# One-hot comparison between gapped layouts, six value buffers and earlier turned blocks in a graph-network kernel

## The chip, the cores and the metric

The kernel runs on one core of a Trainium2 chip. The metric is device time in microseconds (us) of the whole launch, as the median of several executions. Engines are named as the profile names them: PE is the matrix engine, PEld its weight load, DVE the vector engine, ACT the scalar engine, POOL the GpSimd engine, SP the engine that here only issues transfers. SPq and ACTq are transfers issued from SP and ACT.

## The reference, cut to what matters

Four graph layers follow one another on a graph of N = 3125 nodes (feature width 256) and E = 50000 edges. Each layer sums messages over the edges and is followed by a residual and a layer norm. What the change touches is the preparation for them and the first layer's aggregation:

```python
# layer 0: two weighted sums over the edges
a_in  = segment_sum(feat_in[src]  * iw[:, None], dst, num_segments=N)
a_out = segment_sum(feat_out[dst] * ow[:, None], src, num_segments=N)
# layers 1..3 of the second part: the edge attributes summed by destination
e_msg = edge_attr @ We[l].T + be[l]
agg   = segment_sum(x[src] + e_msg, dst, num_segments=n) * inv_deg
```

The kernel never walks the edges in the layers. It first builds an N x N matrix of cells (edge count, summed `iw`, summed `ow`) in memory and a 128 x N sum of the split edge attributes in PSUM. After that every layer is a dense product with that matrix.

## The kernel before, in words

**Scatter stage.** The 50000 edges are 391 tiles of 128 edges (one per partition), taken in chunks of EC = 8 tiles. For each tile ACT compares cell numbers with the neighbouring tiles (`distance`, `equal`), PE finds which edge leads its cell and sums the weights (`claim`, `sums`), and DVE turns eight tiles' sums into values and addresses (`values`, L1299 to L1302). POOL then issues one indirect transfer per tile that adds 128 three-number values to cell_mat (L504); it waits for the landing of the transfer two before. The values lie in VALS = 4 buffers: `values(c)` waits until the scatters of chunk c - 4 have landed.

Edge attributes are summed beside this, LAG = 8 * LAG_C = 40 tiles behind. For tile t, DVE writes a one-hot row per edge (`one_hot`, L1314): 3125 two-byte numbers compared with the edge's destination, into one of three buffers. PE multiplies the 128 attribute columns with it in seven matrix products, one for each 512 columns of the result (`attributes`, L880). ACT and DVE split the attributes of a chunk into a high and a low half (L609, L1308), and `earlier` (L1290) prepares a mask. On each engine all of this is one program in order, so a DVE that waits in `values` writes no one-hots meanwhile.

Before the first one-hot, DVE needs the largest edge attribute: at t = PEAK_SLOT it reads all attributes once in 14 loads (L1332, L1333), and at SCALE_SLOT it forms the scale.

The comparison reads `iota16` through a 125 x 25 view and writes `onehot` through a 25 x 125 view. Both are contiguous, and the profile shows each as one row of 3125.

**Weighted pass.** It starts when every scatter has landed and the attribute sums have been copied from PSUM (`s_ready`). The matrix is read in seven column ranges r (six of 500 columns, one of 125) and 25 row tiles t, 175 steps n. For each step:

- SP loads the cells (L372) into one of three buffers; the load of step n + 3 waits for `lo_ready` of step n. It also stores the counts (L379).
- ACT writes the high half of the weights (`hi_ready`, L651), DVE the low half (`lo_ready`, L1380), POOL casts the counts (L513).
- PE does `in_part` (six products L924 and one L927 for the degrees) and `turns` (eight transposes of blocks into PSUM, L935); `step_done` comes after the last of them.
- ACT copies the turned blocks out of PSUM into `outw` (`turned`, L642).

Every four steps (at t % 4 == 3 and at the last t) a group of turned blocks is complete, and in the next step PE runs `out_part`, a burst of 24 products (L910) on `outw`. DVE adds its result (`added`, L1360 or L1363). There is one `outw`. In program order, ACT does hi(n) and then turned(n - 1); PE does in_part(n), out_part of the pending group, turns(n).

**Later stages.** They are dense products with the count matrix (L1030) and small projections (L978) from about 2100 us on. The change does not touch them.

Of the kernel before, what the change touches and what calls it, by code (L numbers as in the profile page):

```python
# [7 lines left out]
F16 = mybir.dt.float16  # L8
# [3 lines left out]
ALU = mybir.AluOpType  # L12
ACT = mybir.ActivationFunctionType
AX = mybir.AxisListType

P = 125
EPS = 1e-5
WIDE = 4
# [10 lines left out]
def build_gnn(nc, x, src, dst, edge_attr, edge_w, edge_w2, gamma0, beta0, W_in, b_in, W_out, b_out, W_x2i, b_x2i,  # L29
              W_h2h, Wl, bl, Wr, We, be, W_pre, b_pre, W1, b1, W2, b2, W_post, b_post, W3, b3, gamma3, beta3, out):  # L30
    N, D = x.shape
    NT = N // P
# [3 lines left out]
    ET = EM + 1  # L36
    CH = -(-ET // EC)
    in_chunk = lambda c: min(EC, ET - EC * c)
    COLS = WIDE * P
    LAYERS = Wl.shape[0]  # L40
    RANGES = [(r * WIDE, min(WIDE, NT - r * WIDE)) for r in range(-(-NT // WIDE))]
    NR = len(RANGES)
# [13 lines left out]

    LAG_C = 5
    LAG = EC * LAG_C
    VALS = 4
    AHEAD = EC + 4  # L60
    PEAK_LOADS = 13
    PEAK_TILES = EM // PEAK_LOADS
    PEAK_SLOT, SCALE_SLOT = 30, 31

    IN_STEPS = [(r, t) for r in range(NR) for t in range(NT)]
    NS = len(IN_STEPS)
# [22 lines left out]
    with ExitStack() as ctx:  # L89
# [127 lines left out]
        qo = XW + 8 * P  # L217
        iota16 = Q[:, qo:qo + (N + 1) // 2].bitcast(F16)[:, 0:N]
        qe = qo + (N + 1) // 2
        src_i, dst_i = (Q[:, qe + i * ETP:qe + (i + 1) * ETP].bitcast(I32) for i in range(2))  # L220
# [12 lines left out]
        before = [Q[:, qe + s * EC * 64:qe + (s + 1) * EC * 64].bitcast(BF16).rearrange("p (k n) -> p k n", k=EC) for s in range(2)]  # L233
        OH = (N + 1) // 2
        onehot = [AR[:, s * OH:(s + 1) * OH].bitcast(F16)[:, 0:N] for s in range(3)]
        peak_buf = [AR[:, s * PEAK_TILES * EA:(s + 1) * PEAK_TILES * EA] for s in range(2)]
# [5 lines left out]
        apart = [AR[:, ao + s * 192:ao + (s + 1) * 192].bitcast(BF16) for s in range(2)]  # L242
        attr_acc = [psum[:, b, 0:min(512, N - 512 * b)] for b in range(-(-N // 512))]
        ded = lambda c: psum[:, 7, (c % 2) * 128:(c % 2) * 128 + 128]
# [224 lines left out]
        def _(pool):  # L469
# [12 lines left out]
            pool.wait_ge(S["iota_ready"], 1)  # L482
            pool.tensor_copy(iota16, iota_f).then_inc(S["iota_ready"], 1)

# [32 lines left out]
        def _(act):  # L517
# [117 lines left out]
            act.wait_ge(S["attr_done"], ET)  # L635
            act.activation(SA[:, 0:2048].rearrange("p (b n) -> p b n", b=4), psum[:, 0:4, :], ACT.Copy, scale=unscale_a).then_inc(S["s_ready"], 1)

            def turned(n):
                r, t = IN_STEPS[n]
                nt, tt = RANGES[r][1], t % WIDE  # L640
                act.wait_ge(S["step_done"], n + 1)
                act.activation(outw[:, 0:nt, :, tt * P:(tt + 1) * P], turn[n % 2][:, 0:nt], ACT.Copy).then_inc(S["turned"], 1)  # L642
                if t == NT - 1:
                    c0, w = RANGES[r][0] * P, nt * P
                    act.activation(ain[:, :, c0:c0 + w], in_acc[:, :, 0:w], ACT.Copy, scale=unscale0).then_inc(S["in_read"], 1)
            for n, (r, t) in enumerate(IN_STEPS):
                w = RANGES[r][1] * P
                act.wait_ge(cells_in[n % 3], 32 * (n // 3 + 1))
                if n >= 3:
                    act.wait_ge(S["step_done"], n - 2)  # L650
                act.activation(split[n % 3][:, 0, :, 0:w], cells[n % 3][:, 0:3 * w].rearrange("p (n c) -> p c n", c=3)[:, 1:3],  # L651
                               ACT.Copy, scale=scale0[0:P, 1:2]).then_inc(S["hi_ready"], 1)
                if n:
                    turned(n - 1)
            turned(NS - 1)

# [124 lines left out]
        def _(pe):  # L781
# [91 lines left out]
            def attributes(t):  # L873
                c, k = divmod(t, EC)
                if k == 0:
                    pe.wait_ge(S["attr_lo"], c + 1)
                pe.wait_ge(S["onehot_ready"], t + 1)
                own_attr = attr16[c % 2][:, k].rearrange("p c a -> p (c a)")
                for b, a in enumerate(attr_acc):
                    last = pe.matmul(a, own_attr, onehot[t % 3][:, 512 * b:512 * b + a.shape[1]], start=t == 0, stop=t == ET - 1, skip_group_check=True)  # L880
                last.then_inc(S["attr_done"], 1)
# [47 lines left out]
            def turns(n):  # L929
                r, t = IN_STEPS[n]  # L930
                if n >= 2:
                    pe.wait_ge(S["turned"], n - 1)
                for k in range(RANGES[r][1]):
                    for c in range(2):
                        last = pe.transpose(turn[n % 2][:, k, c], split[n % 3][:, c, 1, k * P:(k + 1) * P], ident16[0:P, 0:P])  # L935
                return last
# [5 lines left out]
            for n, (r, t) in enumerate(IN_STEPS):  # L942
                pe.wait_ge(S["lo_ready"], n + 1)
                if t == 0:
                    if pending is not None:
                        out_part(pending)
                    turns(n)
                    in_part(n).then_inc(S["step_done"], 1)
                else:
                    in_part(n)  # L950
                    if pending is not None:
                        out_part(pending)
                    turns(n).then_inc(S["step_done"], 1)
                pending = None
                if t % WIDE == WIDE - 1 or t == NT - 1:
                    pending = groups
                    groups += 1
# [188 lines left out]
        def _(dve):  # L1146
# [164 lines left out]
            def one_hot(t):  # L1311
                if t >= 3:
                    dve.wait_ge(S["attr_done"], t - 2)
                dve.tensor_scalar(onehot[t % 3].rearrange("p (a b) -> p a b", a=N // P), iota16.rearrange("p (a b) -> p a b", a=P), dst_c[:, t:t + 1], None,  # L1314
                                  ALU.is_equal).then_inc(S["onehot_ready"], 1)

# [33 lines left out]
            dve.wait_ge(S["attr_done"], ET)  # L1350
            dve.tensor_scalar(SA[:, 2048:3072].rearrange("p (b n) -> p b n", b=2), psum[:, 4:6, :], unscale_a, None, ALU.mult)
            dve.tensor_scalar(SA[:, 3072:N], psum[:, 6, 0:N - 3072], unscale_a, None, ALU.mult).then_inc(S["s_ready"], 1)

# [23 lines left out]
            for n, (r, t) in enumerate(IN_STEPS):  # L1377
                w = RANGES[r][1] * P
                dve.wait_ge(S["hi_ready"], n + 1)
                dve.scalar_tensor_tensor(out=split[n % 3][:, 1, :, 0:w], in0=cells[n % 3][:, 0:3 * w].rearrange("p (n c) -> p c n", c=3)[:, 1:3],  # L1380
                                         scalar=scale0[0:P, 1:2], in1=split[n % 3][:, 0, :, 0:w], op0=ALU.mult, op1=ALU.subtract).then_inc(S["lo_ready"], 1)
                if (t % WIDE == 1 and t > 1) or (t in (0, 2) and r):
                    added(done)
                    done += 1
                if t == 0 and r:
                    dve.wait_ge(S["step_done"], n)
                    degree(r - 1, False)
# [202 lines left out]
```

## Time and profile before

| What | Value |
|---|---|
| Median of 3 runs | 3545.93 us (3543.48 to 3553.56) |
| The profiled execution's own time | 3530.15 us |
| Its span | 3528.4 us |
| Granted PE clock over the span | 0.893 |
| Busy: PE, DVE, ACT, POOL | 2604.3, 1387.0, 1246.5, 941.1 us |
| Scatter stage, one-hots running | 433.0 to 1349.1 us |
| Weighted pass, six ranges of 500 columns | 1349.1 to about 2056 us |

Starts are microseconds from the start of the span. No engine is busy for most of the span, so the table says little by itself; what matters is what each stage waits for.

### The profile page before, as it was taken

The numbers are of one execution on the slowest core, as the hardware profiler recorded it, in microseconds if no ns is written. First come the engines' busy times: TensorE is split into PE (matmuls) and PEld (weight loads), VectorE is DVE, ScalarE is ACT, GpSimd is POOL, SyncE is SP. The second block draws the span as 40 slices with busy tenths as digits, with TensorE's granted clock in tenths as the row PEclk, the third lists the DMA queues.
The fourth block names the chain that finished last, engine by engine and source line by source line (L and its number), as shares of the span: only waits on it lengthen the run. The fifth ranks groups of instructions, "written<-read, shape, count | busy, mean of one in ns | idle before, by whom it ended". The sixth has DMA issues, their size and how long they took to land. (4 is left out here: it accounts for less than half of the span.)

```text
span 3528.4 us, 36950 instructions
## 1 busy us (share of the span) xinstructions
PE 2604.3 (74%) x14593; PEld 1401.2 (40%) x14593; DVE 1387.0 (39%) x1848; ACT 1246.5 (35%) x2535; POOL 941.1 (27%) x611
## 2 busy tenths in 40 slices
PE   1540096766666775777777769799899996999896
PEld 1310042333332332434444434356555663555543
DVE  2440775545554562444444444401212224133313
ACT  0135195555555514555555541200101112112203
POOL 3000487777777783222222210000000000000000
PEclk9875598888888898999999989899999997999997
DMA  9999633232232226777777752443444424554362
GB/s 377 400 393 396 177 75 53 43 53 43 43 51 45 34 13 144 191 182 186 176 188 193 190 126 68 105 102 80 107 95 93 86 52 104 121 104 105 74 143 74
DMA packets 326008, 466.24 MB, mean 132 GB/s; under 512 B 106089, under 2 KB 261992, under 8 KB 325604
## 3 DMA queue, kind: packets, MB, share of 16 engines
q1 hardware_dynamic: 246445, 420.30, 45.0%
q0 software_dynamic: 57360, 0.92, 4.3%
q10 hardware_dynamic: 22023, 42.59, 3.3%
q8 instruction: 117, 1.92, 0.2%
q14 instruction: 63, 0.52, 0.0%
HBM read 313.97 MB, written 149.75 MB: 131 GB/s over the span
## 5 line engine op out<-in xcount | busy, mean ns | idle before, releaser
L504 POOL DMA_INDIRECT cell_mat<-ROW x391 | 753.0, 1926 | 565.8 <-DMA cell_mat<-SA 322.7
L1030 PE MATMUL psum<-FR 125*128 125x500 f16 (+1 forms) x4200 | 825.9, 355 | 40.5 <-DVE FR L1531 20.8
L880 PE MATMUL psum<-AR,Q 128*128 128x512 f16 (+1 forms) x2737 | 638.3, 385 | 247.0 <-DVE AR L1314 244.1
L1030 PEld LDWEIGHTS psum<-FR 125*128 125x128 f16 x4200 | 388.3, 98 | 451.8 <-issue 69.1
L880 PEld LDWEIGHTS psum<-AR,Q 128*128 128x128 f16 x2737 | 254.4, 104 | 542.3 <-DVE AR L1314 254.3
L1314 DVE TENSOR_SCALAR AR<-Q,ROW 128x3125 f16<-128x3125 f16 x391 | 417.1, 1082 | 94.7 <-PE psum L880 85.6
L924 PE MATMUL psum<-Q,FR 125*128 125x500 f16 (+1 forms) x1050 | 252.1, 381 | 180.9 <-DVE Q L1380 180.9
L1380 DVE SCALAR_TENSOR_TENSOR Q<-Q,small 125x1000 f16<-125x1000 f32 (+1 forms) x175 | 252.4, 1446 | 290.0 <-ACT Q L651 289.7
L1447 DVE SCALAR_TENSOR_TENSOR Q<-psum,small,ROW 128x1000 f32<-128x1000 f32 (+1 forms) x42 | 48.2, 1148 | 747.8 <-PE psum L1030 747.8
L513 POOL CAST Q<-Q 125x500 f16<-125x500 f32 (+1 forms) x175 | 160.4, 916 | 593.5 <-DMA Q<-cell_mat 589.5
L978 PE MATMUL psum<-wl,Q 128*125 128x256 f32 (+1 forms) x1100 | 286.8, 401 | 5.7 <-ACT Q L696 3.0
L642 ACT ACTIVATE Q<-psum 125x1000 f16<-125x1000 f16 (+1 forms) x175 | 160.6, 918 | 326.1 <-PE psum L935 318.2
L651 ACT ACTIVATE Q<-Q,small 125x1000 f16<-125x1000 f32 (+1 forms) x175 | 260.1, 1486 | 44.3 <-DMA Q<-cell_mat 44.1
L586 ACT ACTIVATE AR<-AR,ROW 128x384 bf16<-128x384 f32 x391 | 235.1, 601 | 12.3 <-DMA AR<-cell_rows 11.8
L978 PEld LDWEIGHTS psum<-wl,Q 128*125 128x125 f32 x1100 | 197.7, 188 | 62.4 <-issue 25.5
L910 PE MATMUL psum<-Q,FR 125*128 125x500 f16 (+1 forms) x1050 | 208.9, 354 | 10.0 <-ACT Q L642 6.9
L626 ACT ACTIVATE ROW<-psum 128x1 f32<-128x1 f32 x391 | 63.0, 161 | 420.6 <-PE psum L856 416.1
L924 PEld LDWEIGHTS psum<-Q,FR 125*128 125x128 f16 x1050 | 93.7, 105 | 276.7 <-DVE Q L1380 197.6
L594 ACT ACTIVATE AR<-AR 128x384 bf16<-128x384 bf16 x391 | 198.6, 508 | 0.0
L684 ACT ACTIVATE Q<-psum 128x1000 f32<-128x1000 f32 (+1 forms) x35 | 32.0, 914 | 377.5 <-PE psum L1057 377.5
L910 PEld LDWEIGHTS psum<-Q,FR 125*128 125x128 f16 x1050 | 96.1, 98 | 113.7 <-issue 12.9
L935 PEld LDWEIGHTS psum<-ident,Q 125*125 125x125 f16 x1250 | 106.9, 149 | 64.1 <-issue 39.4
(271 smaller groups left out, 2354.6 us busy)
## 6 DMA issues: line engine op xcount, KB each, us to landing
cell_mat<-SA SPq DMA_DIRECT2D x39, 3000.0 KB, 31.4
Q<-cell_mat SPq DMA_DIRECT2D x150, 703.1 KB
FR<-count_mat SPq DMA_DIRECT2D x180, 585.9 KB
AR<-cell_rows ACTq DMA_DIRECT2D x47, 640.0 KB
count_mat<-Q SPq DMA_DIRECT2D x150, 117.2 KB
AR<-in_edge_attr SPq DMA_DIRECT2D x13, 960.0 KB, 4.7
Q<-in_edge_attr SPq DMA_DIRECT2D x48, 256.0 KB
cell_mat<-ROW POOLq DMA_INDIRECT x391
```

Of the source, the lines that this page charges most:

```text
L504: pool.indirect_dma_start(out=cell_mat, out_offset=bass.IndirectOffsetOnAxis(ap=at[c % VALS][:, k:k + 1], axis=0), in_=vals[c % VALS][:, k ...
L586: act.activation(apart[t % 2].rearrange("p (j n) -> p j n", j=3), rows[c % 2][:, k:k + 3], ACT.Abs, bias=cell_neg[:, t:t + 1]).then_inc(S[ ...
L594: act.activation(same[c % 3][:, k], apart[t % 2].rearrange("p (j n) -> p j n", j=3), ACT.Relu, bias=1.0, scale=-1.0).then_inc(S["eq_done"], 1)
L642: act.activation(outw[:, 0:nt, :, tt * P:(tt + 1) * P], turn[n % 2][:, 0:nt], ACT.Copy).then_inc(S["turned"], 1)
L651: act.activation(split[n % 3][:, 0, :, 0:w], cells[n % 3][:, 0:3 * w].rearrange("p (n c) -> p c n", c=3)[:, 1:3], ACT.Copy, scale=scale0[0 ...
L880: last = pe.matmul(a, own_attr, onehot[t % 3][:, 512 * b:512 * b + a.shape[1]], start=t == 0, stop=t == ET - 1, skip_group_check=True)
L910: last = pe.matmul(out_acc[:, hh, 0:ws], feat[1][:, t0 + k, c, f], outw[:, k, d, 0:ws], start=k == 0 and q == 0, stop=k == nt - 1 and q == ...
L924: pe.matmul(in_acc[:, hh, 0:w], feat[0][:, t, c, f], split[n % 3][:, d, 0, 0:w], start=t == 0 and q == 0, stop=t == NT - 1 and q == 2, ski ...
L978: last = pe.matmul(o, a[:, k * P:(k + 1) * P], wt, start=q == 0, stop=bias is None and q == len(ops) - 1)
L1030: last = pe.matmul(a[:, hh, 0:w], parts[:, c, t, f], slot(m, j)[:, i_, :], start=t == 0 and c == 0, stop=t == NT - 1 and c == 1, skip_grou ...
L1314: dve.tensor_scalar(onehot[t % 3].rearrange("p (a b) -> p a b", a=N // P), iota16.rearrange("p (a b) -> p a b", a=P), dst_c[:, t:t + 1], None,
L1380: dve.scalar_tensor_tensor(out=split[n % 3][:, 1, :, 0:w], in0=cells[n % 3][:, 0:3 * w].rearrange("p (n c) -> p c n", c=3)[:, 1:3], scalar ...
```

## The change

It has four parts.

1. `iota16` is laid out as 125 rows of 25 numbers with a pitch of 26, and each `onehot` buffer as 25 rows of 125 numbers with a pitch of 126. The comparison reads one and writes the other in one instruction of the same 3125 elements. The views can no longer be taken as one row. PE reads the one-hots as rows of 125, so its seven products have 500, ..., 500, 125 columns in place of 512, ..., 512, 53, and the copies out of PSUM follow.
2. VALS goes from 4 to 6 and LAG_C from 5 to 6 (LAG from 40 to 48 tiles).
3. PEAK_SLOT and SCALE_SLOT go from 30, 31 to 37, 38.
4. In the weighted pass PE does the turns of a step ahead of the pending burst. ACT copies turned blocks out one step later, after hi(n) those of step n - 2, and the first copy of a group waits for `out_mm`, the end of the burst that reads `outw`. DVE's `added` moves from t % 4 == 1 to t % 4 == 2.

```diff
-    LAG_C = 5
+    LAG_C = 6
-    VALS = 4
+    VALS = 6
-    PEAK_SLOT, SCALE_SLOT = 30, 31
+    PEAK_SLOT, SCALE_SLOT = 37, 38
...
-        iota16 = Q[:, qo:qo + (N + 1) // 2].bitcast(F16)[:, 0:N]
+        GAP = NT + 1
+        iota16 = Q[:, qo:qo + P * GAP // 2].bitcast(F16).rearrange("p (a b) -> p a b", b=GAP)[:, :, 0:NT]
...
-        OH = (N + 1) // 2
-        onehot = [AR[:, s * OH:(s + 1) * OH].bitcast(F16)[:, 0:N] for s in range(3)]
+        OH = NT * (P + 1) // 2
+        onehot = [AR[:, s * OH:(s + 1) * OH].bitcast(F16).rearrange("p (a b) -> p a b", b=P + 1)[:, :, 0:P] for s in range(3)]
...
-        attr_acc = [psum[:, b, 0:min(512, N - 512 * b)] for b in range(-(-N // 512))]
+        attr_acc = [psum[:, b, 0:nt * P] for b, (_, nt) in enumerate(RANGES)]
...
             def turned(n):
                 act.wait_ge(S["step_done"], n + 1)
+                if tt == 0 and n:
+                    act.wait_ge(S["out_mm"], r * NR + t // WIDE)
...
-                if n:
-                    turned(n - 1)
-            turned(NS - 1)
+                if n >= 2:
+                    turned(n - 2)
+            for n in (NS - 2, NS - 1):
+                turned(n)
...
-                for b, a in enumerate(attr_acc):
-                    last = pe.matmul(a, own_attr, onehot[t % 3][:, 512 * b:512 * b + a.shape[1]], start=t == 0, stop=t == ET - 1, skip_group_check=True)
+                for a, (t0, nt) in zip(attr_acc, RANGES):
+                    last = pe.matmul(a, own_attr, onehot[t % 3][:, t0:t0 + nt], start=t == 0, stop=t == ET - 1, skip_group_check=True)
...
                 if t == 0:
+                    turns(n)
                     if pending is not None:
                         out_part(pending)
-                    turns(n)
                     in_part(n).then_inc(S["step_done"], 1)
                 else:
                     in_part(n)
+                    turns(n).then_inc(S["step_done"], 1)
                     if pending is not None:
                         out_part(pending)
-                    turns(n).then_inc(S["step_done"], 1)
...
-                dve.tensor_scalar(onehot[t % 3].rearrange("p (a b) -> p a b", a=N // P), iota16.rearrange("p (a b) -> p a b", a=P), dst_c[:, t:t + 1], None,
-                                  ALU.is_equal).then_inc(S["onehot_ready"], 1)
+                dve.tensor_scalar(onehot[t % 3], iota16, dst_c[:, t:t + 1], None, ALU.is_equal).then_inc(S["onehot_ready"], 1)
...
-                if (t % WIDE == 1 and t > 1) or (t in (0, 2) and r):
+                if (t % WIDE == 2 and t > 2) or (t in (0, 2) and r):
```

## Rows read from the trace of the kernel before

**Rows 1.** Busy time by stage: time, each engine, clock, DMA share, GB/s

```profile
433.00:1349.10 916.10, 646.04 (x4151) 300.56 (x4151) 501.50 (x665) 500.66 (x1485) 715.33 (x367) 0.85 0.30 45
1349.10:2056.00 706.90, 525.16 (x3212) 282.91 (x3213) 310.28 (x211) 380.56 (x305) 152.63 (x153) 0.95 0.76 188
```

**Rows 2.** Waits between engines, 433 to 1330 us: total us, times, longest

```profile
DVE ROW L1299 <- DMA cell_mat<-ROW: 226.5, 38, 9.8
POOL cell_mat L504 <- DMA cell_mat<-ROW: 97.6, 50, 4.0
...
DVE AR L1314 <- PE psum L880: 85.6, 164, 3.1
DVE Q L1308 <- ACT Q L609: 58.7, 37, 1.8
```

**Rows 3.** Groups of instructions, 433 to 1330 us: busy us, mean ns

```profile
L504 POOL DMA_INDIRECT cell_mat<-ROW x358 | 701.9, 1961 | 224.7 <-DMA cell_mat<-ROW 97.6 <-issue 95.8 <-DVEq L1303 31.4
...
L1314 DVE TENSOR_SCALAR AR<-Q,ROW 128x3125 f16<-128x3125 f16 x391 | 417.1, 1082 | 94.7 <-PE psum L880 85.6 <-issue 0.5
...
L1308 DVE SCALAR_TENSOR_TENSOR Q<-Q,small 128x512 f16<-128x512 f32 x47 | 36.0, 766 | 68.2 <-ACT Q L609 58.7 <-issue 9.5
...
L1290 DVE TENSOR_TENSOR Q<-AR,ROW 128x1024 bf16<-128x1024 bf16 x43 | 29.4, 683 | 0.2 <-PE psum L871 0.2
```

**Rows 4.** POOL in order of time: start us, us, idle before and its releaser

```profile
351.19 1.69 POOL L504 DMA_INDIRECT cell_mat<-ROW  x1 [322.68 <-DMA cell_mat<-SA]
...
402.55 1.54 POOL L504 DMA_INDIRECT cell_mat<-ROW  x1 [1.04 <-DMA cell_mat<-ROW]
432.49 2.56 POOL L504 DMA_INDIRECT cell_mat<-ROW  x1 [28.41 <-DVEq L1303]
...
1345.84 1.54 POOL L504 DMA_INDIRECT cell_mat<-ROW  x1 [0.30 <-issue]
1355.57 0.83 POOL L513 CAST Q<-Q 125x500 f16<-125x500 f32 x1 [8.19 <-DMA Q<-cell_mat]
```

**Rows 5.** DVE in order of time, same columns

```profile
353.22 2.15 DVE L1332 TENSOR_REDUCE small<-AR 128x1 f32<-128x1920 f32 x1 [48.29 <-DMA AR<-in_edge_attr]
...
460.88 4.04 DVE L1314 TENSOR_SCALAR AR<-Q,ROW 128x3125 f16<-128x3125 f16 x4
...
1324.59 1.04 DVE L1314 TENSOR_SCALAR AR<-Q,ROW 128x3125 f16<-128x3125 f16 x1 [0.28 <-PE psum L880]
1328.58 1.28 DVE L1351 TENSOR_SCALAR SA<-psum,small 128x1024 f32<-128x1024 f32 x1 [2.96 <-PE psum L880]
```

**Rows 6.** PE in order of time: one tile's seven attribute products

```profile
803.54 1.50 PE L880 MATMUL psum<-AR,Q 128*128 128x512 f16 x7
...
819.39 2.79 PE L880 MATMUL psum<-AR,Q 128*128 128x512 f16 x7 [8.07 <-DVE AR L1314]
```

**Rows 7.** SP's first loads of the weighted pass, in order of time

```profile
1349.13 2.46 SPq L372 DMA_DIRECT2D Q<-cell_mat  x6
```

**Rows 8.** All engines around one burst, in order of time

```profile
1510.41 1.57 DVE L1380 SCALAR_TENSOR_TENSOR Q<-Q,small 125x1000 f16<-125x1000 f32 x1 [0.70 <-ACT Q L651]
...
1511.26 5.24 PE L910 MATMUL psum<-Q,FR 125*128 125x500 f16 x24
...
1516.34 0.62 PE L935 MATMUL psum<-ident,Q 125*125 125x125 f16 x8
...
1516.79 1.43 PE L924 MATMUL psum<-Q,FR 125*128 125x500 f16 x6
1516.99 1.01 ACT L642 ACTIVATE Q<-psum 125x1000 f16<-125x1000 f16 x1 [6.62 <-PE psum L935]
1517.90 1.62 ACT L651 ACTIVATE Q<-Q,small 125x1000 f16<-125x1000 f32 x1
...
1521.70 0.66 SPq L372 DMA_DIRECT2D Q<-cell_mat  x2
...
1527.83 0.85 POOL L513 CAST Q<-Q 125x500 f16<-125x500 f32 x1 [7.46 <-DMA Q<-cell_mat]
```

**Rows 9.** Busy time in a stretch without pause and in one range, columns as above

```profile
1360.00:1376.00 16.00, 11.24 (x65) 5.57 (x64) 6.50 (x5) 11.44 (x9) 3.73 (x5) 0.95 0.96 250
1477.00:1594.00 117.00, 88.33 (x522) 47.13 (x523) 50.36 (x35) 60.54 (x50) 24.85 (x24) 0.93 0.76 187
```

More of the change, by code:

```diff
@@ L217, in build_gnn @@
         qo = XW + 8 * P
-        iota16 = Q[:, qo:qo + (N + 1) // 2].bitcast(F16)[:, 0:N]
-        qe = qo + (N + 1) // 2
+        GAP = NT + 1
+        iota16 = Q[:, qo:qo + P * GAP // 2].bitcast(F16).rearrange("p (a b) -> p a b", b=GAP)[:, :, 0:NT]
+        qe = qo + P * GAP // 2
         src_i, dst_i = (Q[:, qe + i * ETP:qe + (i + 1) * ETP].bitcast(I32) for i in range(2))
@@ L482, in _ @@
             pool.wait_ge(S["iota_ready"], 1)
-            pool.tensor_copy(iota16, iota_f).then_inc(S["iota_ready"], 1)
+            pool.tensor_copy(iota16, iota_f.rearrange("p (a b) -> p a b", b=NT)).then_inc(S["iota_ready"], 1)
             pool.dma_start(gamma_b, gamma0.unsqueeze(0).to_broadcast([P, D])).then_inc(S["norm_in"], 16)
@@ L635, in _ @@
             act.wait_ge(S["attr_done"], ET)
-            act.activation(SA[:, 0:2048].rearrange("p (b n) -> p b n", b=4), psum[:, 0:4, :], ACT.Copy, scale=unscale_a).then_inc(S["s_ready"], 1)
+            act.activation(SA[:, 0:4 * COLS].rearrange("p (b n) -> p b n", b=4), psum[:, 0:4, 0:COLS], ACT.Copy, scale=unscale_a).then_inc(S["s_ready"], 1)
             def turned(n):
@@ L1350, in _ @@
             dve.wait_ge(S["attr_done"], ET)
-            dve.tensor_scalar(SA[:, 2048:3072].rearrange("p (b n) -> p b n", b=2), psum[:, 4:6, :], unscale_a, None, ALU.mult)
-            dve.tensor_scalar(SA[:, 3072:N], psum[:, 6, 0:N - 3072], unscale_a, None, ALU.mult).then_inc(S["s_ready"], 1)
+            dve.tensor_scalar(SA[:, 4 * COLS:6 * COLS].rearrange("p (b n) -> p b n", b=2), psum[:, 4:6, 0:COLS], unscale_a, None, ALU.mult)
+            dve.tensor_scalar(SA[:, 6 * COLS:N], psum[:, 6, 0:N - 6 * COLS], unscale_a, None, ALU.mult).then_inc(S["s_ready"], 1)
             def added(i):
```

## The prediction, as it was put on record before the changed kernel ran

> **What bounds the kernel now.** I read the busy time by stage first, then the waits, then the engines in order of time where a wait begins and ends. Two stages touched by the change take 916 and 707 us, and no engine fills either [rows 1]: in the first PE is busy for 646 us and POOL for 715 us, in the second PE for 525 us and the DMA engines for 0.76 of the time. So both are chains.
>
> In the scatter stage the chain is POOL's. The waits show DVE held for 226.5 us in 38 waits until scatters have landed [rows 2]. It is ahead of POOL by all four value buffers and stands still, writes no one-hots, and PE starves behind it. A scatter costs POOL 1.96 us on average here, and 0.3 us pass before the next [rows 3]. The reader is to see when it is short: beside DVE's plain reductions and once the one-hots are over it takes 1.54 us [rows 4, 5], beside one-hots up to 2.7 us. The one-hots slow POOL down, and POOL holds DVE back.
>
> At the end both sides are close together: the last one-hot starts at 1324.6, the copies out of PSUM at 1328.6 [rows 5], the last scatter at 1345.8 [rows 4], SP's first cell load at 1349.1 [rows 7].
>
> In the weighted pass the rows round a burst show the second chain. PE bursts for 5.24 us from 1511.3; the turns come only after it at 1516.3; ACT, next in its program the copy of those turned blocks, has stood idle for 6.62 us at 1517.0; its next high half starts at 1517.9, SP's next load at 1521.7, and POOL gets no cells for 7.46 us up to 1527.8 [rows 8]. In a stretch without such a pause the DMA engines are at 0.96 of the time, over a whole range at 0.76 [rows 9].
>
> **The comparison's new rate.** The old one-hot streams 3125 elements at a pitch of 1.01 us (4.04 us for four), of which the reduction gives me the fixed part: 1920 elements at one per 1.04 ns are 2.00 us of its 2.15, so 0.15 to 0.2 us are fixed [rows 5]. About 0.82 us for 3125 elements is four times the reduction's rate. The trace has no comparison between unlike layouts. From below: no change, 1.01 us. From above: one element per tick as in the reduction, 3.25 + 0.2 = 3.45 us. Between them stands a two-byte two-input product at two per tick, 1024 elements in 0.683 us [rows 3]; scaled to 3125 with its fixed part once it gives 1.8, scaled wholly 2.08 us. I take 1.90 us: the element type is that of the two-byte product, so its row is the nearest, and I go a little above its lower scaling because rows of 25 have to start 125 times. With the quadruple rate gone I let the slowing of POOL go too, since it shows beside no other DVE operation.
>
> The Trainium skill (Vector Engine (DVE) Microarchitecture Reference, section 5.1 on performance modes) says that the modes which read through two ports want the outermost count even, or odd and equal in source and destination; here it is 125 against 25, so the two-per-tick mode with one port would be left. The same section says that a pair does not span two rows of the source, which would make 13 ticks of a row of 25, 1625 in all, and by that page's rule and an estimate of 0.2 us fixed the one-hot would take 1.89 us. No row here shows either. The skill's page SBUF — State Buffer (who interferes with whom) says that GpSimd is locked out of a port pair for the whole of a two-port instruction; by that rule, the trace's 1.54 against up to 2.7 us agrees, and by the sum below the price would be the same.
>
> **Scatter stage, DVE.** Its busy time in the stage is 501.5 us, of which one-hots are 417.1 [rows 1, 3], so 84 us are the rest. New: 391 x 1.90 = 743, plus 84 = 827 us. The first one-hot starts at the same 433 us (next paragraph), which gives 1260. Of the waits in front, the 226.5 us vanish if POOL keeps up. The 85.6 us on PE [rows 2] vanish, since PE needs 1.50 us for a tile at full clock [rows 6] against 2.1 us between one-hots; the 2.79 us tiles come only after it has stood 8 us without work, which it no longer does. The 58.7 us on ACT's half split [rows 2] shrink, because PE's claim, which ACT waits for, is no longer behind DVE; I leave 10 us for all gaps. Last one-hot ends at 1270, copies done 5 us later (1325.6 to 1330.5 before), SP starts at 1276 in place of 1349.1. Saved: 73 us, taken as 72.
>
> **Does POOL keep up?** At 1.54 + 0.3 a chunk of eight is 14.7 us. Landing waits are 97.6 us over 46 chunks, 2.1 us each [rows 2]; at the shorter pitch I allow 3. So 17.7 us, against DVE's 827 / 49 = 16.9 us. POOL falls behind by under 1 us a chunk, some 36 us or two chunks over the stage, and six value buffers hold that; DVE would be held from about 19 us on. POOL ends near 432.5 + 45 x 17.7 = 1229, ahead of the one-hots.
>
> **Six buffers, longer lag, later peak slot.** POOL did 24 scatters from 351.2 to 404 and then stood 28.4 us [rows 4] while DVE read the peaks and waited for the first attribute load. With the slot seven tiles later a fourth chunk is ready before it, so POOL does eight more at 2.2 us: the idle time falls to 11 us. The peak loads, the scale and the attribute load behind them stay where the transfers put them, so DVE still starts at 433. Those 17 us are POOL's, and POOL no longer ends last: worth nothing here, 17 us if the comparison changes nothing. Eight tiles more of lag are paid at neither end, since all 391 one-hots still start at 433.
>
> **PE's seven products** keep 3125 columns; the rows of 125 with a gap could slow the reading, but 0.6 us a tile are free. The copies out of PSUM are the same size. Both cost nothing under that cover; without it each 0.1 us a tile is 39 us.
>
> **Weighted pass.** Before, a range of 25 steps takes (2056 - 1355.6) / 6 = 116.7 us. The DMA engines move a range in 0.76 x 117 = 89 us, at 0.96 share 92.7 us or 3.71 us a step [rows 9]. PE is busy for 88.3 us of it. Count the new order from the landing of the cells of the step with the burst, call it step 0. Its halves are done at 3.2 (1.62 + 1.55), in_part and turns at 5.4. ACT takes the high half of step 1 at 3.7 and then copies the last turned blocks of the group, which are done at 6.3: the burst now waits for that, 6.4 to 11.6. The new wait on `out_mm` holds ACT's first copy of the next group to 12.6, and queued behind it is the high half of step 3, due at 11.1. It starts 1.5 us late, its low half ends at 15.8, and only then does SP issue the load of step 6. A first load needs 6.4 us (1349.1 to 1355.6) [rows 4, 7], so it lands at 22.2, when it was due at 6 x 3.7 = 22.2. PE catches up with two steps of 2.1 us each after the burst. So the burst hides behind the transfers, narrowly. At a change of range PE waits for two copies and DVE's reciprocal; I keep 6.5 us and add 1. That is 92.7 + 7.5 = 100.2, and 102 with PE this full. (116.7 - 102) x 6 = 88 us saved. `added` one step later waits for the same burst and holds only a low half that is late anyway. The seventh range is short and I count nothing.
>
> If the transfers run at 3.9 us a step (share 0.91), the range is 107 and the gain 58; if they run at 3.6 and PE follows, 105.
>
> **Sum.** 3530.15 - 72 - 88 = 3370 for the profiled execution. The median of the runs shown stands 15.8 us above that execution, so 3386 us.
>
> **Rivals.**
>
> *One element per tick (slower).* The place is L1314. 391 x 3.45 = 1349, plus 84, puts the last one-hot at 1866 and the pass at about 1883, 534 us later. With 88 us back this gives 3992. It decides as soon as the comparison is over about 2.3 us. For it speaks that no row shows this shape; against it, the two-byte product at two per tick.
>
> *The comparison keeps its rate and its hold on POOL.* If gaps change neither, POOL remains the chain and only the 17 us of the earlier start come: 3546 - 17 - 88 = 3441.
>
> *Landings take POOL's place.* Waits of 4.0 us occur already [rows 2]. At 5.3 us a chunk POOL needs 20 us, ends at 432.5 + 45 x 20 = 1332, and the stage gains 15 us: 3443.
>
> *The burst's stall only moves.* If the two new waits on ACT and PE cost 2 us of the 3.6 that a group has to win, the pass gives 30 us: 3444.
>
> **Chances.** Forecast 0.66; one per tick 0.05; rate and hold kept 0.08; landings 0.07; stall moved 0.12; 0.02 for something else without change. The forecast's own bounds are a comparison of 1.8 us (38 us better) and 2.08 us (70 us worse) and a pass of 58 to 105 us. The range 3335 to 3450 holds the forecast but for its worst corner and the three cases near 3443. Within 0.3% (about what a measurement of this kernel can tell from no change, 10.6 us) lies almost nothing: faster 0.93, same 0.02, slower 0.05.
>
> **What would show it.** One-hots of 1.85 to 2.0 us back to back; scatters of 1.54 us beside them; DVE's wait for landings under 20 us; PE's clock near 1.0 through the stage; SP's first cell load at 1265 to 1290. In the pass, no idle time of 6 us on ACT before L642, cells arriving every 3.7 to 3.9 us across bursts, DMA share near 0.88, a range of 100 to 106 us. Wrong would make it: comparisons over 2.3 us, scatters still near 2 us, or ACT standing before the first copy of a group for more than 2 us.

## The result and the profile after

The changed kernel takes 3319.51 us (median of 4 runs, 3316.99 to 3322.47) against 3544.90 us for the kernel before, measured again on the same chip (3543.48 to 3553.56). The ratio is 0.936, with a 95% interval of 0.9342 to 0.9378. The forecast was 3386 us with a range of 3335 to 3450: the direction was right, and the time lies 66.5 us below the forecast and 15.5 us below the range. The profiled execution of the changed kernel took 3316.99 us over a span of 3315.2 us, at a mean granted PE clock of 0.932.

Busy time by stage, with the columns of [rows 1]. The first row is the scatter stage. The second is the weighted pass with its six wide ranges, which end at 1841.6, and the first steps of the seventh. The third is about one range:

```profile
433.00:1243.70 810.70, 620.06 (x4123) 307.95 (x4123) 797.58 (x665) 504.68 (x1459) 571.58 (x361) 0.99 0.34 50
1243.70:1862.50 618.80, 518.82 (x3303) 282.19 (x3303) 314.47 (x222) 390.61 (x316) 148.88 (x156) 0.96 0.84 215
1340.00:1441.00 101.00, 86.05 (x555) 46.67 (x554) 53.38 (x37) 65.89 (x54) 25.15 (x26) 0.98 0.86 221
```

In the scatter stage DVE is now busy for 797.6 of 810.7 us, where before no engine filled the stage [rows 1]. It is no longer a chain but one full engine. The granted clock rose from 0.85 to 0.99. PE's longest wait for a one-hot was 10.2 us before and is 1.1 us now, and its waits for them fell from 244.1 to 174.1 us. In the pass the DMA share went from 0.76 to 0.84, and to 0.86 in the range of the third row.

The two groups of instructions that changed most (busy us, mean ns, idle before):

```profile
L505 POOL DMA_INDIRECT cell_mat<-ROW x391 | 619.6, 1585 | 536.3 <-DMA cell_mat<-SA 323.8
L1318 DVE TENSOR_SCALAR AR<-Q,ROW 128x3125 f16<-128x3125 f16 x391 | 721.4, 1902 | 7.0 <-PE psum L884 0.5
```

A one-hot takes 1902 ns where it took 1082 [rows 3]. A scatter takes 1585 ns; over the whole of the kernel before it took 1926. The slower instruction made the stage faster: DVE's wait for landings, 226.5 us before [rows 2], has no row left, and its wait for PE fell from 85.6 to 0.5 us. What is left of the waits of [rows 2], from 433 to 1349 us:

```profile
POOL cell_mat L505 <- DMA cell_mat<-ROW: 87.8, 68, 3.3
...
DVE Q L1312 <- ACT Q L610: 16.9, 2, 16.3
```

The end of the stage, DVE in order of time (start us, us, idle before). Each row with x8 or x10 is a run of successive one-hots:

```profile
1191.62 14.60 DVE L1318 TENSOR_SCALAR AR<-Q,ROW 128x3125 f16<-128x3125 f16 x8
...
1221.88 18.22 DVE L1318 TENSOR_SCALAR AR<-Q,ROW 128x3125 f16<-128x3125 f16 x10
1241.70 1.26 DVE L1354 TENSOR_SCALAR SA<-psum,small 128x1000 f32<-128x1000 f32 x1 [1.60 <-PE psum L884]
1242.88 0.34 DVE L1355 TENSOR_SCALAR SA<-psum,small 128x125 f32<-128x125 f32 x1
```

POOL, in order of time, is done long before, and SP's first load follows the copies out of PSUM:

```profile
1183.19 1.55 POOL L505 DMA_INDIRECT cell_mat<-ROW  x1 [0.30 <-issue]
1250.00 0.84 POOL L514 CAST Q<-Q 125x500 f16<-125x500 f32 x1 [65.26 <-DMA Q<-cell_mat]
```
```profile
1243.72 2.34 SPq L373 DMA_DIRECT2D Q<-cell_mat  x6
```

**Where the 213 us of span came from.** The profiled spans differ by 3528.4 - 3315.2 = 213.2 us. SP's first load moved from 1349.1 [rows 7] to 1243.7: 105.4 us in the scatter stage. From there to the first projection of the next stage it was 769.0 us and is 661.9 us: 107.1 us in the weighted pass. What follows takes 1410 us in both, to 0.7 us.

Around a burst, all engines in order of time (to compare with [rows 8]):

```profile
1378.87 1.08 POOL L514 CAST Q<-Q 125x500 f16<-125x500 f32 x1 [2.69 <-DMA Q<-cell_mat]
...
1382.42 0.85 POOL L514 CAST Q<-Q 125x500 f16<-125x500 f32 x1 [2.48 <-DMA Q<-cell_mat]
...
1383.61 0.62 PE L939 MATMUL psum<-ident,Q 125*125 125x125 f16 x8
1383.93 1.00 ACT L645 ACTIVATE Q<-psum 125x1000 f16<-125x1000 f16 x1
...
1384.99 5.25 PE L914 MATMUL psum<-Q,FR 125*128 125x500 f16 x24 [0.76 <-ACT Q L645]
...
1386.31 0.87 POOL L514 CAST Q<-Q 125x500 f16<-125x500 f32 x1 [3.04 <-DMA Q<-cell_mat]
...
1390.03 0.86 POOL L514 CAST Q<-Q 125x500 f16<-125x500 f32 x1 [2.85 <-DMA Q<-cell_mat]
...
1390.34 1.02 ACT L645 ACTIVATE Q<-psum 125x1000 f16<-125x1000 f16 x1 [2.41 <-PE psum L914]
...
1391.24 1.63 ACT L654 ACTIVATE Q<-Q,small 125x1000 f16<-125x1000 f32 x1
...
1392.90 1.57 DVE L1383 SCALAR_TENSOR_TENSOR Q<-Q,small 125x1000 f16<-125x1000 f32 x1 [1.37 <-ACT Q L654]
1393.73 1.45 POOL L514 CAST Q<-Q 125x500 f16<-125x500 f32 x1 [2.84 <-DMA Q<-cell_mat]
```

The turns stand ahead of the burst; ACT copies the last turned blocks of the group at 1383.9, and the burst waits 0.76 us for them. While PE is in the burst, POOL goes on receiving cells, at 1386.3, 1390.0 and 1393.7, with no pause of 7 us. ACT does wait for the burst, 2.41 us at 1390.3, and the high half behind it starts at 1391.2. That is the new wait on `out_mm`, and the next cells still come on time.

### The profile page after: what moved, and what is told of

It reads as the page before. It is cut to its first block and busy times, and to the rows that moved or that the text cites. A ratio compares the mean times of both kernels' runs of the same rounds, so it can differ in the third digit from the quotient of the medians.

```text
span 3315.2 us, 37002 instructions
## 1 busy us (share of the span) xinstructions
PE 2562.0 (77%) x14593; PEld 1400.3 (42%) x14593; DVE 1677.6 (51%) x1848; ACT 1262.7 (38%) x2535; POOL 803.3 (24%) x611
## 5 line engine op out<-in xcount | busy, mean ns | idle before, releaser
L505 POOL DMA_INDIRECT cell_mat<-ROW x391 | 619.6, 1585 | 536.3 <-DMA cell_mat<-SA 323.8
L884 PE MATMUL psum<-AR,Q 128*128 128x500 f16 (+1 forms) x2737 | 592.5, 356 | 184.0 <-DVE AR L1318 174.1
L1318 DVE TENSOR_SCALAR AR<-Q,ROW 128x3125 f16<-128x3125 f16 x391 | 721.4, 1902 | 7.0 <-PE psum L884 0.5
L884 PEld LDWEIGHTS psum<-AR,Q 128*128 128x128 f16 x2737 | 237.2, 98 | 455.5 <-DVE AR L1318 175.0
L654 ACT ACTIVATE Q<-Q,small 125x1000 f16<-125x1000 f32 (+1 forms) x175 | 262.2, 1499 | 116.7 <-DMA Q<-cell_mat 116.0
L928 PE MATMUL psum<-Q,FR 125*128 125x500 f16 (+1 forms) x1050 | 238.4, 365 | 77.9 <-DVE Q L1383 76.0
L914 PE MATMUL psum<-Q,FR 125*128 125x500 f16 (+1 forms) x1050 | 210.7, 356 | 22.4 <-ACT Q L645 14.2
L629 ACT ACTIVATE ROW<-SA,ROW 128x9 bf16<-128x9 bf16 x391 | 119.1, 305 | 12.7
```

Of the source, the lines that this page charges most:

```text
L505: pool.indirect_dma_start(out=cell_mat, out_offset=bass.IndirectOffsetOnAxis(ap=at[c % VALS][:, k:k + 1], axis=0), in_=vals[c % VALS][:, k ...
L884: last = pe.matmul(a, own_attr, onehot[t % 3][:, t0:t0 + nt], start=t == 0, stop=t == ET - 1, skip_group_check=True)
L914: last = pe.matmul(out_acc[:, hh, 0:ws], feat[1][:, t0 + k, c, f], outw[:, k, d, 0:ws], start=k == 0 and q == 0, stop=k == nt - 1 and q == ...
L928: pe.matmul(in_acc[:, hh, 0:w], feat[0][:, t, c, f], split[n % 3][:, d, 0, 0:w], start=t == 0 and q == 0, stop=t == NT - 1 and q == 2, ski ...
L1318: dve.tensor_scalar(onehot[t % 3], iota16, dst_c[:, t:t + 1], None, ALU.is_equal).then_inc(S["onehot_ready"], 1)
```

## The experiments

Two theories were open for the scatter stage. Mine: the gaps take the quadruple rate from the comparison, scatters beside it then keep their short duration, and DVE alone sets the stage, so buffers, lag and slot add nothing. The rival: the gaps slow DVE as much as they free POOL, and the deeper buffers carry the gain. For the pass the question was which of its two parts (the order on PE or the later copy on ACT) does the work. Chips differ by up to 14 us (the kernel before took 3530.94 to 3544.90 us on them), so ratios are against the kernel before on the same chip, and within a run I compare places in the span. Such a place moves from trace to trace: with the scatter stage untouched, SP's first load came at 1349.1 [rows 7], 1350.3, 1355.2 and 1356.3, so where POOL is the chain a difference under 7 us says nothing.

**gaps_alone**: the kernel before, with the two gapped layouts, the products per range of columns and the comparison alone. Buffers, lag, slots and the pass as before.

```diff
+iota16 = Q[:, qo:qo + P * GAP // 2].bitcast(F16).rearrange("p (a b) -> p a b", b=GAP)[:, :, 0:NT]
+onehot = [AR[:, s * OH:(s + 1) * OH].bitcast(F16).rearrange("p (a b) -> p a b", b=P + 1)[:, :, 0:P] for s in range(3)]
```

> The kernel before with the gapped layouts alone (four value buffers, lag of 5 chunks, old order in the weighted pass). Theory 1, the comparison's rate holds POOL: one-hots of 1.90 us at a pitch of 1.81 us, scatters of about 1.59 us, DVE the chain at 16.6 us a chunk against POOL's 17.2; three to four chunks of room suffice for that, so SP's first cell load comes at 1244 to 1255 us and the median is 3440 to 3450 us. Theory 2, the depth of the value buffers did it: with four buffers DVE still waits over 150 us for landings, first load after 1320 us, median over 3515 us.

Measured: 3427.29 us against 3538.28, ratio 0.9683 (0.9666 to 0.9699). One-hots 1901 ns, scatters 1595 ns, no wait of DVE for landings. SP's first load:

```profile
1243.55 2.40 SPq L373 DMA_DIRECT2D Q<-cell_mat  x6
```

That is 0.2 us from the place that it has with all parts. The median lies 13 us below the 3440 to 3450 that I expected; 7 of them are the quicker chip, and the rest I can't place. POOL still stood 28.3 us for DVE's values, as in [rows 4], and nothing waited for POOL.

**after_no_gaps**: the changed kernel with contiguous layouts again; buffers, lag, slots and the pass changed.

```diff
-onehot = [... .rearrange("p (a b) -> p a b", b=P + 1)[:, :, 0:P] for s in range(3)]
+onehot = [AR[:, s * OH:(s + 1) * OH].bitcast(F16)[:, 0:N] for s in range(3)]
```

> The changed kernel with both layouts contiguous again, all else changed. Theory 1: one-hots of 1.04 to 1.08 us, scatters of 1.93 to 1.96 us again, POOL the chain, only the eight scatters done earlier (17 us) remain of the stage's gain: first load at 1325 to 1335 us, median 3400 to 3412 us. Theory 2 (depth did it): first load near 1250 us, median 3320 to 3335 us.

Measured: 3406.82 us, ratio 0.9637 (0.9619 to 0.9656). Scatters 1933 ns, one-hots 1083 ns. SP's first load, and DVE's and POOL's waits:

```profile
1333.13 2.52 SPq L372 DMA_DIRECT2D Q<-cell_mat  x6
```
```profile
DVE ROW L1302 <- DMA cell_mat<-ROW: 193.6, 33, 9.1
...
POOL cell_mat L504 <- DMA cell_mat<-ROW: 89.2, 46, 4.1
...
POOL cell_mat L504 <- DVEq L1306: 3.6, 1, 3.6
```

Six buffers still fill up. POOL's wait for the values shrinks from 28.4 us [rows 4] to 3.6, and the stage ends 16 us earlier, because eight scatters are done before the peak reductions are. The two runs settle it: deeper buffers, longer lag and the later slot are together worth 16 us while POOL is the chain (16 to 23 us against the four places above) and nothing once it isn't. The rival falls.

**pass_alone**: the kernel before with the order on PE, the copy one step later on ACT, its wait on `out_mm` and `added` one step later.

> The kernel before with the new order of the weighted pass alone (ACT's copies one step later, turns ahead of the burst). If the pass gains by its own order: scatter stage unchanged (first cell load at 1349 us), a range of 25 steps takes 100 us in place of 117, median 3545 - 107 = 3438 us (3430 to 3446). If the pass was faster only because the scatter stage left PE's clock or the transfers in another state: a range over 108 us and a median over 3480 us.

Measured: 3432.89 us, ratio 0.9701 (0.9684 to 0.9717). First load at 1356.3, DVE's wait for landings still 229.8 us; the ranges after the first take 99.5 to 102.3 us. The two halves add up: (1 - 0.9683) + (1 - 0.9701) = 0.0616, against 0.064 for the whole change, inside the intervals.

**pe_order_alone**: the kernel before, with only this order on PE (and the wait on `out_mm` before ACT's first copy of a group, without which the blocks could be overwritten); ACT still copies one step behind.

```diff
                 else:
                     in_part(n)
+                    turns(n).then_inc(S["step_done"], 1)
                     if pending is not None:
                         out_part(pending)
-                    turns(n).then_inc(S["step_done"], 1)
```

> The kernel before with only PE's order changed (turns ahead of the burst) and the wait for the end of the burst that this needs, but ACT still copying the blocks of step n - 1 after its high half n. By my timeline ACT's first copy of the next group then waits for the burst before the high half of step 2 of the group, about 4 us late, so the stall stays: a range of 112 to 120 us and a median of 3520 to 3560 us. If PE's order alone carried the gain, the range is about 100 us and the median about 3440 us.

Measured: 3544.15 us, ratio 1.002 (1.0008 to 1.0031). Ranges take 112.3 to 118.8 us after the first (110.8 to 120.7 in the kernel before). Around a burst:

```profile
1510.86 5.24 PE L912 MATMUL psum<-Q,FR 125*128 125x500 f16 x24
...
1516.20 1.02 ACT L644 ACTIVATE Q<-psum 125x1000 f16<-125x1000 f16 x1 [5.73 <-PE psum L912]
...
1526.57 0.86 POOL L513 CAST Q<-Q 125x500 f16<-125x500 f32 x1 [5.58 <-DMA Q<-cell_mat]
```

The turned blocks are ready ahead of the burst, at 1511.0, but ACT's next instruction is the copy into `outw`, which the burst is still reading. ACT now stands 5.73 us for the burst where it stood 6.62 for the turns [rows 8], and POOL gets no cells for 5.6 us. The stall only changed its name.

**act_lag_alone**: the kernel before with ACT's side, and with DVE's `added` moved from t % 4 == 1 to t % 4 == 2 as in the whole change. On PE the turns still come after the burst.

```diff
+                if tt == 0 and n:
+                    act.wait_ge(S["out_mm"], r * NR + t // WIDE)
...
-                if n:
-                    turned(n - 1)
-            turned(NS - 1)
+                if n >= 2:
+                    turned(n - 2)
+            for n in (NS - 2, NS - 1):
+                turned(n)
...
-                if (t % WIDE == 1 and t > 1) or (t in (0, 2) and r):
+                if (t % WIDE == 2 and t > 2) or (t in (0, 2) and r):
```

> The kernel before with only ACT's side of the weighted pass changed: copies one step later with their wait for the end of the burst, and DVE's addition one step later; PE keeps the burst ahead of the turns. By my timeline the burst runs from 6.4 to 11.6 us after the cells of its step, the turns follow at 12.1, ACT's first copy of the next group ends at 13.2 instead of 12.6, and the load of step 6 lands 0.6 us late: a range of 100 to 105 us, median 3435 to 3465 us. If both halves of the change are needed: a range over 112 us, median over 3510 us.

Measured: 3432.98 us, ratio 0.9703 (0.9661 to 0.9745), ranges of 98.5 to 101.6 us after the first. I had expected 3435 to 3465 us; the median lies 2 us below. Around a burst:

```profile
1441.71 5.25 PE L913 MATMUL psum<-Q,FR 125*128 125x500 f16 x24 [0.95 <-ACT Q L644]
1443.08 1.64 ACT L653 ACTIVATE Q<-Q,small 125x1000 f16<-125x1000 f32 x1 [1.43 <-DMA Q<-cell_mat]
...
1444.75 1.58 DVE L1383 SCALAR_TENSOR_TENSOR Q<-Q,small 125x1000 f16<-125x1000 f32 x1 [2.42 <-ACT Q L653]
1446.36 0.66 SPq L372 DMA_DIRECT2D Q<-cell_mat  x2
...
1447.00 1.26 DVE L1363 TENSOR_SCALAR AR<-psum,small 128x1000 f32<-128x1000 f32 x1 [0.67 <-PE psum L913]
...
1447.45 1.02 ACT L644 ACTIVATE Q<-psum 125x1000 f16<-125x1000 f16 x1 [2.73 <-PE psum L938]
```

It equals pass_alone. With the copy one step later, ACT has a high half to do inside the burst (1443.1), and what is left of its wait is 2.7 us (2.4 in the changed kernel). DVE follows with its low half at 1444.8 and SP loads at 1446.4, all inside the burst; only then does DVE add the burst's result. With `added` still one step earlier, it would stand ahead of that low half in DVE's program and wait for the burst. No run takes ACT's copy and DVE's addition apart. So the whole gain of the pass belongs to these two together, and the new order on PE is worth nothing, alone or with them.

The next three runs take the changed kernel and give the comparison other rows with the same 3125 elements. They ask what lowers its rate: gaps, unequal numbers of rows, or the source's short rows.

**equal_rows**: the source in 25 rows of 125 with gaps, just as the target.

```diff
-iota16 = ... .rearrange("p (a b) -> p a b", b=GAP)[:, :, 0:NT]
+iota16 = Q[:, qo:qo + NT * (P + 1) // 2].bitcast(F16).rearrange("p (a b) -> p a b", b=P + 1)[:, :, 0:P]
```

> The changed kernel with the source of the comparison laid out as the target is, 25 rows of 125 at a pitch of 126: gaps in both, row counts equal. Theory A, unequal row counts lower the rate: the gaps alone do nothing, one-hots are 1.04 to 1.10 us again, scatters 1.93 us, first cell load near 1333 us, median 3400 to 3412 us (of the kernel with no gaps). Theory B, the gaps lower it: one-hots of 1.90 us, median 3315 to 3325 us.

Measured: 3388.82 us, ratio 0.9592 (0.9563 to 0.9622). The page's groups:

```profile
L505 POOL DMA_INDIRECT cell_mat<-ROW x391 | 727.1, 1860 | 557.1 <-DMA cell_mat<-SA 324.2
...
L1318 DVE TENSOR_SCALAR AR<-Q,ROW 128x3125 f16<-128x3125 f16 x391 | 432.7, 1126 | 82.0 <-PE psum L884 74.2
```

SP's first load:

```profile
1315.01 2.51 SPq L373 DMA_DIRECT2D Q<-cell_mat  x6
```

Gapped rows alone keep the quick rate (1126 ns against 1083 without gaps), and with it come back the long scatters, up to 2.90 us, and DVE's wait for landings, 168.7 us. The gap is not what the change works by. It is not without effect, though: SP's first load came at 1315.0, where I had expected 1333, the place without gaps (1333.1), and the mean scatter is 73 ns shorter than there (1860 against 1933). Why was not tried.

**swapped_rows**: the source in 25 rows of 125, the target in 125 rows of 25. The opposite pair of unlike counts.

> The changed kernel with the two layouts exchanged: the source is 25 rows of 125 (pitch 126), the target 125 rows of 25 (pitch 26), and PE reads the one-hots in rows of 25. If two elements are taken at a time within a row of the source, a row of 25 costs 13 ticks and one of 125 costs 63: 1575 ticks in place of 1625, 52 ns less, one-hots of 1.85 us, the stage 20 us shorter, median 3296 to 3302 us. If the rows of the target count, or neither's: one-hots stay at 1.90 us, median 3315 to 3325 us. If PE is slowed by rows of 25: its seven products take over 1.6 us; up to 1.8 us is hidden, beyond that 39 us for each 0.1 us.

**source_one_row**: the source as one row of 3125, the target in 25 rows of 125 with gaps.

```diff
-iota16 = ... .rearrange("p (a b) -> p a b", b=GAP)[:, :, 0:NT]
+iota16 = Q[:, qo:qo + (N + 1) // 2].bitcast(F16)[:, 0:N].rearrange("p (a b) -> p a b", b=NT)
```

> The changed kernel with the source contiguous (one row of 3125) and the target gapped as changed. If unequal counts lower the rate and pairs are taken within source rows: 1563 ticks, one-hots of 1.84 us, the stage 25 us shorter, median 3291 to 3297 us, scatters at 1.59 us. If one gapped side is not enough to lower the rate: one-hots of 1.04 us, median 3400 to 3412 us.

Measured for swapped_rows 3298.82 us, ratio 0.934 (0.9316 to 0.9364), for source_one_row 3292.48 us, ratio 0.9323 (0.9299 to 0.9347). The comparison in the one and the other:

```profile
L1318 DVE TENSOR_SCALAR AR<-Q,ROW 128x3125 f16<-128x3125 f16 x391 | 701.0, 1849 | 7.5 <-PE psum L884 0.9
```
```profile
L1318 DVE TENSOR_SCALAR AR<-Q,ROW 128x3125 f16<-128x3125 f16 x391 | 696.0, 1836 | 7.2 <-PE psum L884 0.7
```

Both stay at the lower rate, with scatters of 1563 and 1551 ns beside them: unlike numbers of rows lower it. All the counts tried are odd. SP's first load comes at 1224.3 and 1218.2, 19 and 26 us earlier than in the changed kernel, and both medians lie in the ranges expected. What remains depends on the source's rows. DVE's two copies out of PSUM take 1.26 us for 1000 elements and 0.34 us for 125, which is 1.05 ns an element. If that is a tick, two elements go per tick and no pair spans two source rows, then 125 rows of 25 need 1625 ticks, 25 rows of 125 need 1575, one row 1563. The differences to the first would be 52.5 and 65 ns; measured are 53 and 66 ns. The Trainium skill (Vector Engine (DVE) Microarchitecture Reference, section 5.1) states both: an odd outermost count unlike in source and destination shuts out the modes with two ports, and pairs stay inside a row of the source. By that rule, these runs agree.

**mixed_8 and mixed_4**: source_one_row, but every eighth (or fourth) tile writes a contiguous one-hot, which is quick. The question: how much of the quick rate can POOL bear?

```diff
+target = lambda t: (onehot_flat if t % 8 == 7 else onehot)[t % 3]
```

> The changed kernel with a contiguous source, and with a contiguous target as well in every eighth tile (49 tiles), which then runs at the quadruple rate. If DVE bounds the stage and each quick one-hot costs POOL about 0.4 us: DVE wins 49 x 0.8 = 39 us, POOL loses 20 of the some 50 us by which it ends earlier, first cell load near 1182 to 1192 us, some 32 us under the kernel with a contiguous source alone. If POOL is closer to the bound than its end shows: first load over 1205 us.

> The same with every fourth tile (98 tiles) quick. DVE alone would end at 1218 - 78 = 1140 us; POOL, 39 us later than with none, ends at about 1207 us and is the bound: DVE waits for landings again, first cell load 1200 to 1215 us, so slower than every eighth tile. If POOL were not slowed: first load below 1170 us.

Measured for mixed_8 3282.52 us, ratio 0.928 (0.9249 to 0.931), for mixed_4 3330.58 us, ratio 0.9421 (0.9391 to 0.9452). SP's first load in the one and the other:

```profile
1208.60 2.39 SPq L375 DMA_DIRECT2D Q<-cell_mat  x6
```
```profile
1253.58 2.52 SPq L375 DMA_DIRECT2D Q<-cell_mat  x6
```

My expectations (1182 to 1192 and 1200 to 1215) were both missed; for mixed_8 the other case that I had written down came, that POOL is closer to the bound than its end shows (over 1205). I had carried only the longer scatters into the sum, and POOL pays twice. From source_one_row over mixed_8 to mixed_4 the scatters go from 1551 to 1599 to 1644 ns, and their waits for earlier landings, 433 to 1349 us, from 79.7 to 105.2 to 129.3 us. Single scatters reach 2.32 and 2.34 us in the two, against 1.91 in source_one_row. From source_one_row to mixed_8 the end of DVE's copies moves forward from 1217.7 to 1191.3, and POOL's last scatter back from 1166.1 to 1205.4, so POOL is now the side that ends last. In mixed_4 its last scatter starts at 1250.3, and DVE waits 58.9 us for landings. mixed_8 has the lowest time measured, but its interval overlaps that of source_one_row. Its first load is 9.6 us earlier, but its pass took 8.6 us longer in the profiled execution, so that the first projection of the next stage starts only 1.0 us earlier (1879.4 against 1880.3). A gain of mixed_8 over source_one_row is not shown. Nor was it tried why POOL waits longer for landings when DVE is quick.

## Where the prediction was wrong, and what held

Both mechanisms held: a slower comparison that lets POOL go, and a burst that hides behind the transfers. What failed is the sum, in terms that all made the kernel too slow. The one-hots were priced by their duration and not by their pitch (743 us for 721.4). The rest of DVE's work and the copies were 11 us too long. Every wide range was charged 102 us, a change of range included (98.6 measured, 14 us in all). The seventh range and the ends of the pass were put at nothing (5 us). And 15.8 us were added from the profiled execution to the median (2.5 measured). In the pass one step failed outright: the turns ahead of the burst on PE, which the prediction counts as part of the gain, brought none of it.

**One-hots, `391 x 1.90 = 743`: the duration was right, the term wrong.** The comparison took 1902 ns against 1.90 us forecast. But successive one-hots overlap in the records: eight take 14.60 us, which is a pitch of (14.60 - 1.90) / 7 = 1.81 us. The group's row shows it directly, 721.4 us busy for 391 of a mean of 1902 ns, and so did the row before: 417.1 / 391 = 1.067 against a mean of 1.082 [rows 3]. I had used the pitch, 1.01 us, to derive the rate and then the duration to build the sum. This term is 22 us of the miss. The rest of DVE's work, taken as 84, overlaps its neighbours too: 797.6 - 721.4 - 1.6 for the two copies leaves 75, 9 less; the 84 already held 1.5 us of copies, for which the sum paid again behind the last one-hot. The gaps came to about the 10 forecast. So the last one-hot ended at 1240.1 in place of 1270, and with copies 2 us shorter SP started at 1243.7 in place of 1276: 105 us saved where I had taken 72.

**POOL keeps up: right, with more room than I gave.** I forecast 17.7 us a chunk and an end near 1229. From 431.5 to 1183.2 it made 360 steps from scatter to scatter, 2.09 us each or 16.7 us a chunk. I had allowed 3 us a chunk for landings; they took 87.8 / 45 = 2.0. A scatter took 1585 ns and not 1.54 us, which took back 0.4 us a chunk. Six buffers weren't needed for it: gaps_alone has four and no wait. The parts around the gaps were forecast at nothing with them and 17 us without; measured are 0.2 and 16.0 us, and that the second agrees so closely is in part luck, since that place moves by 7 us between traces.

**DVE's other waits: right.** PE 85.6 to 0.5 us, landings 226.5 to 0, half splits 58.7 to 16.9, granted clock 0.99.

**Weighted pass, `100.2, and 102 with PE this full`: mechanism half right, size low.** The burst hides behind the transfers, and at the burst shown above the times of the prediction's count came out: counted from POOL's cast at 1378.9, the burst ran from 6.1 to 11.4 us (forecast 6.4 to 11.6), the late low half ended at 15.6 (15.8). ACT's wait for it (2.4 us) harms nothing, although I had named more than 2 us there as a sign of being wrong; that sign was set too low. But I credited the edits together. The runs show that ACT's later copy, with DVE's later addition, does all of it, and PE's order nothing. As to the size, six ranges took 1841.6 - 1250.0 = 591.6 us by the starts of POOL's casts, 98.6 each and not 102, against (2049.1 - 1355.6) / 6 = 115.6 before by the same count. I had used 116.7, with 2056 as the end. That is 102 us saved and not 88. The first range took 91.2 us, 3.65 a step (forecast 3.71): there is no change of range in front of it, for which I had charged all six. The other five, with one pause of about 11 us each, took 99.3 to 101.0. The remaining 5 us are what I put at nothing: the seventh range and the ends of the pass. In the nine traces in which ACT copies one step later the six ranges took 98 to 100 us each on average, so the miss of the 102 is small but not chance.

**The sum.** Scatter stage 33 us too small, pass 19 us too small: with 0.7 us behind them 53 us against the profiled execution (3370 forecast, 3317 measured). The other 13 us come from the 15.8 that I added to go from the profiled execution to the median of the runs; of the changed kernel the median is only 2.5 above it. The range held a comparison of 1.8 us or a pass gain of 105 us at its low end, each by itself. Both terms came out there at once, which leads to 3333 us, just under the low end of 3335; the 13 us from the median then put the time 15.5 us below it.

**The rivals.** One element per tick: out, the one-hot took 1902 ns. Rate and hold kept: out for this layout, but equal_rows shows it, with a one-hot of 1126 ns and a mean scatter of 1860 ns. Landings in POOL's place: out here (2.0 us a chunk); in mixed_4 they come to 129.3 / 45 = 2.9 us a chunk and, with longer scatters, make POOL last, still far from the 5.3 of the rival. Stall moved: out for the whole change, but it is what PE's order alone does (ranges of 114.5 us on average, 115.6 before).

## What to carry to other kernels

When two engines share a stage, look at what each does to the other's durations: here a comparison 0.8 us slower made the stage 105 us shorter, since the scatters beside it got shorter (1926 to 1585 ns on average) and DVE's waits for them went away. For a sum over a run of like instructions take the pitch (or the group's busy time over its count), never the mean duration, and where a stall comes from an engine's program order, ask of each reordering which engine's next instruction it frees: reordering PE left ACT in front of the same burst, and one step of lag on ACT, with DVE's addition a step later, gave the whole gain.

## What the runs showed of the hardware that I had not expected

- The comparison's rate depended on whether source and target have like numbers of rows (all odd here), and hardly on gaps (1083 ns without them, 1126 with): 25 against 25 rows with gaps 1126 ns, 125 against 25 rows 1902, 25 against 125 rows 1849, one against 25 rows 1836.
- The scatters beside it are hardly lengthened by the lower rate (1551 to 1595 ns on average) and much by the higher one (1860 to 1933, single ones up to 2.90 us). Already one quick comparison in eight adds 48 ns to the mean scatter and 26 us of waits for landings.
- PE's products ran no slower on one-hots in rows of 125 with gaps: seven took 1.50 us at full clock [rows 6], and still did afterwards (1.54 to 1.56 us on rows of 25 in swapped_rows). In order of time:

```profile
793.03 1.50 PE L884 MATMUL psum<-AR,Q 128*128 128x500 f16 x7 [0.21 <-DVE AR L1318]
```
